# Twelve normalisations of a four-layer transformer kernel moved from blocks of their own into the blocks of the stages that read them

## The chip, the cores and the metric

The kernel runs on one core of one Trainium2 chip. The metric is the device time of one execution in microseconds (us), as the median of several runs. A core has five engines that run side by side and meet only at semaphores: TensorE (PE, with PEld for its weight loads), VectorE (DVE), ScalarE (ACT), GpSimd (POOL) and SyncE (SP), which here only issues DMA transfers.

## The reference

The input is x, 4 batches of 512 tokens with 128 channels, and a context of 154 tokens per batch. Four layers each add a cross attention and then a second part to x, and every such part reads a layer norm of x:

```python
def _layernorm(x, axis=-1, eps=1e-05):
    m = jnp.mean(x, axis=axis, keepdims=True)
    v = jnp.var(x, axis=axis, keepdims=True)
    return (x - m) / jnp.sqrt(v + eps)
...
x = x + _L0_xattn_ref(_layernorm(x, axis=-1), ctx_1024, itok_BxS_0_511, ...)
x = x + _L0_ffn_ref(_layernorm(x, axis=-1), ...)
```

The second part of layer 0 is a causal attention behind a convolution and a mixture of experts, each with one more layer norm (with gain and bias) in front. That of layer 1 is a soft decision tree. That of layer 2 is a latent attention and a mixture of experts, each behind an RMS norm with a gain. That of layer 3 is a product of 8-bit quantised matrices. This makes twelve norms.

## The kernel before

The whole of x lies in on-chip memory as X, with channels on the 128 partitions and 4 x 512 tokens along the free dimension. The norms write Y and Z of the same shape. All of it is float32. The program is a row of phases: input, window attention (names L0x), convolution and causal attention (L0f), experts (L0m), cross attention (L1x), tree (L1f), cross attention (L2x), latent heads (L2f), experts (L2m), attention over heads (L3x) and output.

Each phase is one `nc.Block`: an instruction stream for every engine, in the order in which it is written (or in which the phase's own order list `S.order` puts its steps). At its end `Phase.done` (L111) drains the engines, clears the phase's semaphores and makes all engines meet at a barrier. No scheduler moves instructions: each engine takes its stream in order and stops at the first wait that isn't met.

A norm is such a phase too, `phase_norm` (L179 to L253), which the stage calls through `norm((ld, loads))` just ahead of its own block. It works on four batches of 512 columns, one after the other on each engine:

- PE multiplies the source by a matrix of 1/128 (`mean`), L203, which leaves every token's mean in all partitions of banks 0 to 3 of the accumulator P. DVE subtracts it (L213).
- The squares are made by POOL (L242) for batches 0 and 2 and by DVE (L216, or L219 where nothing is centred) for 1 and 3. PE averages them (L206) into banks 4 to 7.
- ACT takes the logarithm of all four (L249), loads another function table, and takes exp(-0.5 x) of all four (L252).
- DVE multiplies (L227; L229 with a gain; L232 and L234 with gain and bias). Only when the last batch is done does the block end.

SP issues the weights of the following stage in the norm's block (`fetch`). The first norms of L0f and L2f are called from `build` and fetch nothing, so there the weights come with the second norm.

The stage's own block starts behind that barrier. What stands first in it, and is named below: in L0x, PE folds weights (L1196 on). In L0f, DVE clears tiles (L959, L960) and then starts the convolution (L968). In L0m and L2m, PE runs the router (L2147), 16 tiles of tokens with 4 or 8 outputs, DVE clears `hp` (L2209) and reads the logits (L2211, L2215). In L1x and L2x, POOL prepares the context (L526 to L529), DVE clears tiles and scales a bias (L652 to L658), and PE makes keys and values (L563, L564) and then queries (L556), which DVE reads at L677 and L665. In L1f, PE folds weights (L2305), ACT copies them (L2348), and PE multiplies Y by the copy (L2314). In L2f, PE folds weights (L1533, L1539), ACT copies them (L1629, L1631), and PE starts on Z (L1545), whose result DVE reads at L1674. In L3x, POOL clears tiles and ACT reads the keys and values (L2624) and queries (L2634). In the output phase, PE transposes Z (L2733) and DVE takes maxima (L2786).

Of the kernel before, what the change touches and what calls it, by code (L numbers as in the profile page):

```python
# [178 lines left out]
def phase_norm(nc, G, name, src, dst, center=True, gain=None, bias=None, fetch=None, sq=None):  # L179


    ph = Phase(nc, name)
    P = G["P"]
    xc = dst if center else src
    sq = rs = ph.sb("sq", [128, NB, T]) if sq is None else sq
    step, ld = ph.count("step"), ph.count("ld")
    given = [v for v in (gain, bias) if v is not None]
    cols = [ph.sb(f"col{n}", [128, 1]) for n in range(len(given))]
    gain, bias = ([c[:, 0:1] for c in cols] + [None, None])[:2]
    mean_up, cent, squared, squared_by_dve, var_up, ln, rstd, out = (  # L190
        ph.count(n) for n in ("mean_up", "cent", "squared", "squared_by_dve", "var_up", "ln", "rstd", "out"))
    with nc.Block() as block:
        @block.sync
        def _(sp):
            load_all(sp, ld, [(c[:], v) for c, v in zip(cols, given)])
            if fetch:
                load_all(sp, *fetch)

        @block.tensor
        def _(pe):  # L200
            if center:
                for b in range(NB):
                    nc.tensor.matmul(P[:, b, :], G["mean"][:], src[:, b, :], start=True, stop=True).then_inc(*mean_up.up())  # L203
            for b in range(NB):
                pe.wait_ge(*(squared_by_dve if b % 2 else squared).at(0, b // 2 + 1))
                nc.tensor.matmul(P[:, 4 + b, :], G["mean"][:], sq[:, b, :], start=True, stop=True).then_inc(*var_up.up())  # L206

        @block.vector
        def _(dve):
            if center:  # L210
                for b in range(NB):
                    dve.wait_ge(*mean_up.at(0, b + 1))
                    nc.vector.tensor_tensor(xc[:, b, :], src[:, b, :], P[:, b, :], ALU.subtract).then_inc(*cent.up())  # L213
                    if b % 2:
                        dve.wait_ge(*cent.at(0, b + 1))
                        nc.vector.tensor_tensor(sq[:, b, :], xc[:, b, :], xc[:, b, :], ALU.mult).then_inc(*squared_by_dve.up())  # L216
# [2821 lines left out]
```

## Time and profile before

| | us |
|---|---|
| median of 3 runs | 1771.7 |
| lowest and highest | 1768.62 and 1781.09 |
| the profiled execution | 1771.55 |
| its span, from its first to its last instruction | 1769.7 |

The mean granted clock of PE over that span is 0.873 of full speed.

So 1.85 us lie outside the span. The profile's page gives busy times per engine and the costliest groups. For this change the timeline is the view to read: it lists instructions by start and duration, with the time for which the engine had been idle and what it had waited for in brackets.

### The profile page before, as it was taken

The numbers are of one execution on the slowest core, as the hardware profiler recorded it, in microseconds if no ns is written. First come the engines' busy times: TensorE is split into PE (matmuls) and PEld (weight loads), VectorE is DVE, ScalarE is ACT, GpSimd is POOL, SyncE is SP. The second block draws the span as 40 slices with busy tenths as digits, with TensorE's granted clock in tenths as the row PEclk, the third lists the DMA queues.
The fourth block names the chain that finished last, engine by engine and source line by source line (L and its number), as shares of the span: only waits on it lengthen the run. The fifth ranks groups of instructions, "written<-read, shape, count | busy, mean of one in ns | idle before, by whom it ended". The sixth has DMA issues, their size and how long they took to land. (4 is left out here: it accounts for less than half of the span.)

```text
span 1769.7 us, 23757 instructions
## 1 busy us (share of the span) xinstructions
PE 1417.7 (80%) x8978; PEld 724.7 (41%) x8980; DVE 1041.1 (59%) x1468; ACT 704.1 (40%) x1306; POOL 572.9 (32%) x594
## 2 busy tenths in 40 slices
PE   5868755788858999699668986699999657689984
PEld 3345522333333444344234434354554232256553
DVE  3698736677642222578366752466676145468866
ACT  2444431666720000277334753244444221255522
POOL 1477713453302110332113301634422100047660
PEclk7789986899969999889886996899999669879986
DMA  3000010000010000100010002000000000000000
GB/s 102 0 1 0 1 44 1 1 1 1 1 75 0 0 0 0 50 1 1 9 49 1 1 1 44 1 1 1 2 2 1 1 29 0 6 1 1 2 1 26
DMA packets 19154, 20.58 MB, mean 12 GB/s; under 512 B 9803, under 2 KB 15163, under 8 KB 18408
## 3 DMA queue, kind: packets, MB, share of 16 engines
q1 hardware_dynamic: 18024, 19.07, 3.5%
q8 instruction: 71, 1.16, 0.3%
q14 instruction: 35, 0.29, 0.0%
q10 hardware_dynamic: 1024, 0.07, 0.0%
HBM read 17.94 MB, written 1.05 MB: 11 GB/s over the span
## 5 line engine op out<-in xcount | busy, mean ns | idle before, releaser
L1663 ACT ACTIVATE L2f_prob<-P 128x512 f32<-128x512 f32 x160 | 86.8, 595 | 112.6 <-PE P L1601 112.6
L998 DVE TENSOR_REDUCE L0f_nm<-P 128x2 f32<-128x768 f32 (+3 forms) x88 | 97.2, 1121 | 42.7 <-PE P L904 42.5
L2174 PE MATMUL P<-L0m_hm,L0m_w 128*128 128x512 f32 x256 | 112.5, 600 | 2.6 <-POOL L0m_hm L2136 2.6
L1691 DVE TENSOR_REDUCE L2f_nm<-P 128x2 f32<-128x768 f32 (+3 forms) x88 | 99.2, 1128 | 3.0
L1601 PE MATMUL P<-L2f_qs,L2f_ks 49*128 49x384 f32 (+3 forms) x512 | 94.3, 477 | 7.7 <-ACT L2f_prob L1663 3.9
L954 ACT ACTIVATE L0f_prob<-P 128x512 f32<-128x512 f32 x160 | 87.3, 601 | 29.4 <-PE P L917 26.9
L1517 POOL TENSOR_SCALAR_AFFINE_SELECT L2f_prob<-L2f_prob 128x512 f32<-128x512 f32 x64 | 39.7, 635 | 168.1 <-ACT L2f_prob L1663 168.0
L1690 DVE TENSOR_TENSOR P<-P,L2f_mask 128x256 f32<-128x256 f32 (+2 forms) x88 | 48.4, 550 | 74.3 <-PE P L1587 73.1
L1587 PE MATMUL P<-L2f_ks,L2f_qs 48*128 48x384 f32 (+3 forms) x512 | 87.7, 451 | 3.4 <-DVE L2f_nm L1691 3.4
L2516 POOL TENSOR_TENSOR L3x_exm<-L3x_exm,L3x_rec 128x2048 f32<-128x2048 f32 x16 | 72.3, 4526 | 26.1 <-DVE L3x_rec L2690 26.1
L2174 PEld LDWEIGHTS P<-L0m_hm,L0m_w 128*128 128x128 f32 x256 | 49.2, 193 | 64.9 <-issue 62.8
L1246 PE MATMUL P<-ident,L0x_pv 128*128 128x128 f32 x384 | 53.5, 305 | 24.4 <-POOL L0x_pv L1164 24.4
L1601 PEld LDWEIGHTS P<-L2f_qs,L2f_ks 49*128 49x128 f32 x512 | 49.4, 197 | 55.3 <-issue 41.4
L2198 ACT ACTIVATE L0m_ex<-P 128x512 f32<-128x512 f32 x16 | 9.6, 597 | 155.9 <-PE P L2174 155.9
L1154 POOL TENSOR_TENSOR L0x_prod<-L0x_qs,L0x_kg 128x1536 f32<-128x1536 f32 x20 | 68.5, 3454 | 3.3 <-ACT L0x_qs L1290 3.3
L1350 DVE TENSOR_REDUCE L0x_sc<-L0x_prod 128x16 f32<-128x1536 f32 x40 | 68.1, 1744 | 2.0 <-POOL L0x_prod L1154 1.9
L867 POOL TENSOR_SCALAR_AFFINE_SELECT L0f_prob<-L0f_prob 128x512 f32<-128x512 f32 x64 | 39.6, 637 | 88.6 <-ACT L0f_prob L954 88.6
L2251 DVE SCALAR_TENSOR_TENSOR L0m_rc<-L0m_ex,P 128x512 f32<-128x512 f32 x16 | 11.0, 688 | 95.0 <-ACT L0m_ex L2198 95.0
L2182 PE MATMUL P<-L0m_act,L0m_w 128*128 128x512 f32 x128 | 59.3, 623 | 9.2 <-DVE L0m_act L2254 9.2
L2574 PE MATMUL P<-L3x_exm,ident 128*128 128x512 f32 x128 | 62.5, 634 | 3.0 <-DVE L3x_rec L2690 1.9
L2136 POOL TENSOR_TENSOR L0m_hm<-Z,L0m_me 128x512 f32 x16 | 20.5, 1309 | 137.1 <-DVE L0m_act L2254 107.2
L1246 PEld LDWEIGHTS P<-ident,L0x_pv 128*128 128x128 f32 x384 | 51.3, 218 | 31.4 <-POOL L0x_pv L1164 29.7
(575 smaller groups left out, 3298.7 us busy)
## 6 DMA issues: line engine op xcount, KB each, us to landing
L0m_w<-in_L0m_w SPq DMA_DIRECT2D x1, 2048.0 KB, 7.7
L0f_va<-in_L0f_va SPq DMA_DIRECT2D x3, 512.0 KB, 4.7
in_xt<-in_x SPq DMA_DIRECT2D x1, 1024.0 KB
L0x_segi<-in_segb SPq DMA_DIRECT2D x1, 1024.0 KB, 5.0
L0m_w<-in_L0m_w SPq DMA_DIRECT2D x1, 1024.0 KB, 9.7
out<-out_o SPq DMA_DIRECT2D x4, 256.0 KB, 2.5
L1x_va<-in_va SPq DMA_DIRECT2D x3, 256.0 KB, 3.1
L1x_vr<-in_vr SPq DMA_DIRECT2D x3, 256.0 KB, 4.3
```

The lines of the kernel that those rows point to most:

```text
L954: nc.scalar.activation(S.group_prob(b, g)[:, slot, :], P[:, bank, :], ACT.Exp).then_inc(*S.act_done.up())
L998: nc.vector.tensor_reduce(S.nm[:, qt, first:first + 2 * many].rearrange("p (i e) -> p e i", e=2), P[:, bank:bank + 2, 0:many * width].rear ...
L1154: ops.tensor_tensor(prod[(k - 1) % S.NPROD][:], q, kg[b % 3][:, qt, j, :].unsqueeze(1).to_broadcast([128, H, 96]), ALU.mult)\
L1246: m = mm(P[:, bank, g * 128:(g + 1) * 128], pv[(4 * b + n) % 2][:, j, 4 * g:4 * g + 4, :].rearrange("p h c -> p (h c)"), G["ident"][:], st ...
L1350: nc.vector.tensor_reduce(sc[b % 2][:, n[0], n[1], :], prod[(S.place["prod", b, n] - 1) % S.NPROD][:], AX.X, ALU.add)\
L1587: m = mm(P[:, bank + e, p * width:(p + 1) * width], S.qs[b % 2][64 * e:64 * e + 48, pair, qt * 128:(qt + 1) * 128], S.ks[b % 2][64 * e:64 ...
L1601: m = mm(P[:, banks[e], at:at + width], S.ks[b % 2][64 * e:64 * e + 49, kt * 128:(kt + 1) * 128], S.qs[b % 2][64 * e:64 * e + 49, pair, q0 ...
L1663: nc.scalar.activation(S.group_prob(b, g)[:, slot, :], P[:, bank, :], ACT.Exp).then_inc(*S.act_done.up())
L1691: nc.vector.tensor_reduce(S.nm[:, qt, first:first + 2 * many].rearrange("p (i e) -> p e i", e=2), P[:, bank:bank + 2, 0:many * width].rear ...
L2174: m = mm(P[:, bank, :], lhs, hm[:, e, :], start=e == 0, stop=e == E - 1)
L2516: nc.gpsimd.tensor_tensor(ex[:], ex[:], S.rec[u % 2][:].unsqueeze(1).to_broadcast([128, H, 128]), ALU.mult).then_inc(*S.p_ready.up())
L2574: m = mm(P[:, 4, :], G["ident"][:], S.ex_of(b, n)[:, 8 * e + 4 * i:8 * e + 4 * i + 4, :].rearrange("p h q -> p (h q)"), start=e + i == 0, ...
```

## The change

`phase_norm` is gone. A class `Norm` holds the same instructions as methods, one for each engine (for DVE two: `dve_first` up to the squares, `dve_last` for the final products), and `Norms` runs one or two of them in a row. The stage calls these at the head of its own streams, so that the block end, the clearing of semaphores and the barrier between norm and stage no longer exist: 12 of 23 such meetings. What the barrier kept apart is now kept apart by waits: PE waits for all four logarithms (`N.ln`) before it writes an accumulator bank for the stage, and for `N.out` of batch b before its first step on that batch. Where a stage has two norms, the second's source waits per batch for the first's output, and they use two scratch tiles.

Some preparations move ahead of, or in between, the norm's parts:

- L0f: the clearing of tiles stands between `dve_first` and `dve_last` of the second norm.
- L0m, L2m: the clearing of `hp` likewise.
- L1x, L2x, L3x: POOL prepares the context before its squares. DVE clears tiles between `dve_first` and `dve_last`. In L1x and L2x its wait for all loads and the scaling of a bias stand there too.
- L0x: the one-hot tables, with their wait for the loads, stand between DVE's two parts.
- L2f: PE folds the weights between the two norms, ACT copies them there, and the loads are issued ahead of both norms.

```diff
-def phase_norm(nc, G, name, src, dst, center=True, gain=None, bias=None, fetch=None, sq=None):
...
-            dve.wait_ge(*out.at(0, NB))
...
-    ph.done()
+class Norm:
...
+    def source(self, eng, b):
+        if self.before is not None:
+            eng.wait_ge(self.before.out.sem, b + 1)
...
+class Norms:
...
+    def on_pe(self, pe):
+        for n in self.all:
+            n.on_pe(pe)
...
+    def dve_first(self, dve):
+        for n in self.all[:-1]:
+            n.dve_first(dve)
+            n.dve_last(dve)
+        self.all[-1].dve_first(dve)
+
+    def dve_last(self, dve):
+        self.all[-1].dve_last(dve)
```

In `phase_cross` (L1x and L2x), and in the same way in the other stages:

```diff
-    norm((ld, loads))
+    N = Norms(ph, G, norm)
     head_of = lambda g, j: 8 * (g // 2) + 2 * j + g % 2
     with nc.Block() as block:
+        @block.sync
+        def _(sp):
+            N.on_sp(sp)
+            load_all(sp, ld, loads)
...
             nc.gpsimd.tensor_copy(ctr[:], ctp[:, :, 128:PAD].unsqueeze(2).to_broadcast([128, NB, 4, 32])).then_inc(*ready.up())
+            N.on_pool(pool)
...
+            N.on_pe(pe)
             mm = nc.tensor.matmul
             pe.wait_ge(ld.sem, 16 * len(loads))
+            pe.wait_ge(N.ln.sem, NB)
             for s in S.order:
                 kind, b, n = s
                 if kind == "q":
+                    pe.wait_ge(N.out.sem, b + 1)
...
+            N.dve_first(dve)
             for t in S.qx:
                 nc.vector.memset(t[:, :, :, 48:64].rearrange("p t h c -> p (t h) c"), 0.0).then_inc(*cleared.up())
...
             dve.wait_ge(ld.sem, 16 * len(loads))
             link(dve, nc.vector.tensor_scalar(bq[:], bq[:], 8.0 ** -0.5, None, ALU.mult), step)
+            N.dve_last(dve)
```

In `phase_latent_heads` (L2f) and in `build`:

```diff
+            N.all[0].on_pe(pe)
             pe.wait_ge(ld.sem, 16 * len(loads))
...
             m.then_inc(*pre_full.up())
+            N.all[1].on_pe(pe)
+            pe.wait_ge(N.ln.sem, NB)
             for s in S.order:
                 kind, b, n = s
+                if kind in ("k", "p", "lat"):
+                    pe.wait_ge(N.out.sem, b + 1)
...
-        phase_norm(nc, G, "n2f", X, Y)
-        phase_latent_heads(nc, G, D, lambda fetch, sq: phase_norm(nc, G, "n2a", Y, Z, center=False, gain=D["L2_w_ln1"], fetch=fetch, sq=sq))
+        phase_latent_heads(nc, G, D, [(X, Y, {}), (Y, Z, {"center": False, "gain": D["L2_w_ln1"]})])
```

PE's stream at the start of L2f before, where `L2f_prob` is the second norm's scratch and the branches are the ends and starts of blocks:

```order
L203 MATMUL P<-X,mean 128x512 x4
L206 MATMUL P<-n2f_sq,mean 128x512 x4
L192 UNCONDITIONAL_BRANCH
L199 UNCONDITIONAL_BRANCH
L206 MATMUL P<-L2f_prob,mean 128x512 x4
L192 UNCONDITIONAL_BRANCH
L1529 UNCONDITIONAL_BRANCH
L1533 MATMUL P<-L2f_turned,L2f_qk 128x16 x16
L1539 MATMUL P<-L2f_qk,L2f_turned 32x128 x16
L1545 MATMUL P<-Z,L2f_wka 128x512
```

And the same place after the change, where L207, L1608, L1614 and L1624 are the new numbers of L206, L1533, L1539 and L1545:

```order
L204 MATMUL P<-X,mean 128x512 x4
L207 MATMUL P<-L2f_prob,mean 128x512 x4
L1608 MATMUL P<-L2f_turned,L2f_qk 128x16 x16
L1614 MATMUL P<-L2f_qk,L2f_turned 32x128 x16
L207 MATMUL P<-L2f_prob,mean 128x512 x4
L1624 MATMUL P<-Z,L2f_wka 128x512
```

The folding of the weights has moved from behind the second norm to the front of it, and four branches are gone.

DVE's stream at the start of L1x before, with L216 the squares of the norm and L227 its final products:

```order
L216 TENSOR_TENSOR n1x_sq<-Y 128x512
L227 TENSOR_TENSOR Y<-Y,n1x_sq 128x512 x4
L192 UNCONDITIONAL_BRANCH
L649 UNCONDITIONAL_BRANCH
L652 MEMSET L1x_qx 128x64x8 x2
...
L656 MEMSET L1x_kx 26x16x16
L658 TENSOR_SCALAR L1x_bq<-L1x_bq 128x128
L677 TENSOR_TENSOR L1x_xk<-P,L1x_bk 128x256
```

And after the change, where L237 and L248 are the squares and the products, and L698, L702, L704 and L724 the former L652, L656, L658 and L677:

```order
L237 TENSOR_TENSOR L1x_n0sq<-Y 128x512
L698 MEMSET L1x_qx 128x64x8 x2
...
L702 MEMSET L1x_kx 26x16x16
L704 TENSOR_SCALAR L1x_bq<-L1x_bq 128x128
L248 TENSOR_TENSOR Y<-Y,L1x_n0sq 128x512 x4
L724 TENSOR_TENSOR L1x_xk<-P,L1x_bk 128x256
```

The stage's preparations, with the wait for the loads that stands ahead of the scaling of `bq`, have moved in between the norm's squares and its products.

## Rows read from the trace of the kernel before

**Rows 1.** The page, first part: engine, busy us (share of the span), number of instructions.
```profile
PE 1417.7 (80%) x8978; PEld 724.7 (41%) x8980; DVE 1041.1 (59%) x1468; ACT 704.1 (40%) x1306; POOL 572.9 (32%) x594
```

**Rows 2.** Timeline, start of L0f: start us, duration us, engine, line, operation [idle before <-releaser].
```profile
245.76 6.23 PE L203 MATMUL P<-Y,mean 128*128 128x512 f32 x8 [6.20 <-PEq L111]
...
258.20 0.75 DVE L232 SCALAR_TENSOR_TENSOR Z<-Z,n0a_col,L0f_prob 128x512 f32<-128x512 f32 x1 [4.67 <-ACT L0f_prob L252]
...
264.15 0.48 DVE L959 MEMSET L0f_qk<- 128x512 uint32 x1 [1.13 <-PEq L111]
...
267.24 0.36 DVE L968 TENSOR_SCALAR L0f_hb<-Z,L0f_conv 128x512 f32<-128x512 f32 x1
```

**Rows 3.** Windows: stretch us, its length, busy of each engine, granted PE clock, DMA share, GB/s.
```profile
507.00:513.00 6.00, 0.00 (x0) 0.01 (x1) 4.68 (x8) 1.66 (x4) 0.00 (x0) 0.50 0.00 0
716.00:728.50 12.50, 7.24 (x16) 2.88 (x16) 6.77 (x10) 7.50 (x10) 2.08 (x2) 1.00 0.54 174
...
1087.00:1099.00 12.00, 11.33 (x67) 9.52 (x68) 0.35 (x1) 0.74 (x2) 1.90 (x2) 0.50 0.00 1
```

**Rows 4.** Timeline of PEld, start of L0x.
```profile
27.55 0.63 PEld L1196 LDWEIGHTS P<-L0x_wkT,L0x_wqT 64*48 64x48 f32 x7 [6.99 <-DMA L0x_kidx<-in_kidx]
```

**Rows 5.** Timeline, start of L0m.
```profile
507.20 0.75 DVE L232 SCALAR_TENSOR_TENSOR Z<-Z,n0m_col,n0m_sq 128x512 f32<-128x512 f32 x1 [4.74 <-ACT n0m_sq L252]
...
513.12 6.99 PE L2147 MATMUL P<-L0m_router,Z 128*128 128x4 f32 x32
520.47 0.91 DVE L2209 MEMSET L0m_hp<- 128x1024 uint32 x1 [7.16 <-PE P L2147]
```

**Rows 6.** Timeline, start of L1x.
```profile
721.54 1.38 SPq L130 DMA_DIRECT2D L1x_vr<-in_vr  x3
...
726.11 2.50 DVE L227 TENSOR_TENSOR Y<-Y,n1x_sq 128x512 f32<-128x512 f32 x4 [4.19 <-ACT n1x_sq L252]
...
731.13 1.19 PE L563 MATMUL P<-L1x_wkv,L1x_ctp 128*128 128x256 f32 x2 [7.72 <-POOL L1x_ctr L529]
...
733.29 0.42 DVE L677 TENSOR_TENSOR L1x_xk<-P,L1x_bk 128x256 f32<-128x256 f32 x1 [0.86 <-PE P L564]
```

**Rows 7.** DMA issues: tile, queue, count, KB each, median us to landing.
```profile
L1x_vr<-in_vr SPq DMA_DIRECT2D x3, 256.0 KB, 4.3
```

**Rows 8.** Timeline of ACT, start of L1f.
```profile
874.08 0.37 ACT L2348 COPY L1f_gw<-P 128x255 f32<-128x255 f32 x1 [3.19 <-PE P L2305]
```

**Rows 9.** Timeline, start of L2f.
```profile
1057.31 1.28 ACT L249 ACT_TABLE_LOAD   x1 [9.51 <-PEq L111]
...
1073.55 0.33 SPq L130 DMA_DIRECT2D n2a_col<-in_L_w_ln  x1
...
1074.67 6.51 PE L206 MATMUL P<-L2f_prob,mean 128*128 128x512 f32 x8 [7.27 <-POOL L2f_prob L242]
...
1082.34 1.39 SPq L130 DMA_DIRECT2D L2f_va<-in_L2f_va  x3
...
1083.95 2.74 DVE L229 SCALAR_TENSOR_TENSOR Z<-Y,n2a_col,L2f_prob 128x512 f32<-128x512 f32 x4 [7.34 <-ACT L2f_prob L252]
...
1087.67 6.98 PE L1533 MATMUL P<-L2f_turned,L2f_qk 32*128 32x16 f32 x32 [6.49 <-PEq L111]
...
1094.58 1.95 PE L1539 MATMUL P<-L2f_qk,L2f_turned 32*32 32x128 f32 x32
...
1098.64 0.69 DVE L1674 TENSOR_TENSOR L2f_ks<-P,L2f_ck 128x512 f32<-128x512 f32 x1 [11.95 <-PE P L1545]
```

**Rows 10.** Timeline of DVE, start of L2m.
```profile
1425.31 2.74 DVE L229 SCALAR_TENSOR_TENSOR Z<-Y,n2m_col,n2m_sq 128x512 f32<-128x512 f32 x4 [7.32 <-ACT n2m_sq L252]
...
1437.45 0.29 DVE L2215 TENSOR_TENSOR L2m_lg<-P,L2m_ebias 128x128 f32<-128x128 f32 x1
```

**Rows 11.** Timeline of ACT, start of L3x.
```profile
1553.12 0.37 ACT L2624 COPY L3x_xk<-P 128x256 f32<-128x256 f32 x1 [6.75 <-POOL L3x_va L2504]
```

**Rows 12.** Timeline of DVE, start of the output phase.
```profile
1744.63 0.69 DVE L2786 TENSOR_REDUCE out_amax<-P 128x4 f32<-128x512 f32 x1 [2.12 <-PE P L2733]
```

More of the change, by code:

```diff
@@ new lines, with __init__, on_sp, on_pe @@
+class Norms:
+    def __init__(self, ph, G, specs, sq=()):
+        self.all = []
+        for i, (src, dst, kinds) in enumerate(specs):
+            self.all.append(Norm(ph, G, src, dst, sq=sq[i] if sq else None, before=self.all[-1] if i else None, tag=f"n{i}", **kinds))
+        self.out, self.ln = self.all[-1].out, self.all[-1].ln
+    def on_sp(self, sp):
+        for n in self.all:
+            load_all(sp, n.ld, n.loads)
+    def on_pe(self, pe):
+        for n in self.all:
+            n.on_pe(pe)
+    def on_pool(self, pool):
+        for n in self.all:
+            n.on_pool(pool)
+    def on_act(self, act):
+        for n in self.all:
+            n.on_act(act)
+    def dve_first(self, dve):
+        for n in self.all[:-1]:
+            n.dve_first(dve)
+            n.dve_last(dve)
+        self.all[-1].dve_first(dve)
+    def dve_last(self, dve):
+        self.all[-1].dve_last(dve)
@@ L848, in phase_conv_attention, with _ @@
              (mask[:], D["mask_q"])] + [(t[:], D["L0f_va"]) for t in va]
-    norm((ld, loads), sq=S.prob[0][:, 0:NB, :])
+    N = Norms(ph, G, norm, sq=[t[:, 0:NB, :] for t in S.prob[0:2]])
     with nc.Block() as block:
+        @block.sync
+        def _(sp):
+            N.on_sp(sp)
+            load_all(sp, ld, loads)
         @block.gpsimd
         def _(pool):
+            N.on_pool(pool)
             for b, n in ((0, 1),):
@@ L1477, in phase_latent_heads @@
              (ck[:], D["L2f_ck"]), (sk[:], D["L2f_sk"]), (one[:], D["L2f_one"]), (mask[:], D["mask_q"])] + [(t[:], D["L2f_va"]) for t in S.va]
-    norm((ld, loads), sq=S.prob[0][:, 0:NB, :])
+    N = Norms(ph, G, norm, sq=[t[:, 0:NB, :] for t in S.prob[0:2]])
     with nc.Block() as block:
@@ L2125, in phase_experts, with _ @@
     hott_ps = [P[:, 1 + i, :].bitcast(BF16) for i in range(2)]
-    norm((ld, loads))
+    N = Norms(ph, G, norm)
     with nc.Block() as block:
+        @block.sync
+        def _(sp):
+            N.on_sp(sp)
+            load_all(sp, ld, loads)
         @block.gpsimd
         def _(pool):
+            N.on_pool(pool)
             if one:
@@ L2715, in phase_output @@
     tiles = lambda bank: P[:, bank, :].rearrange("p (t c) -> p t c", c=128)
-    norm((ld, loads))
+    N = Norms(ph, G, norm)
     with nc.Block() as block:
```

236 lines of the change are left out of this document (148 added, 88 removed).

## The prediction

> **What bounds the kernel now.** I read the page first, to see that no engine is full: PE is busy for 1417.7 us of the 1769.7 us span, DVE for 1041.1 [rows 1]. So the end is set stage by stage, and what the change is worth must be read where it acts, at the twelve norms. I read the timeline there. At each norm one finds the same serial chain over the engines (mean, subtraction, squares, mean, logarithm, table, exponential, product), then a barrier, then preparations of the stage that need no norm at all, and only then the first work on Y or Z. While the chain runs its four batches, most engines stand still. Last I read the windows for PE's granted clock, since PE's pieces there are short and follow idle time.
>
> The barrier's price is the bracket at the first instruction behind it: 1.13 us on DVE in L0f [rows 2]. Twelve go, about 12 x 1.1 = 13 us. The greater part must be what overlaps once they are gone. I follow, stage by stage, the first instruction of the stage that the rest hangs on, before and after. All of a stage is one pipeline behind it, so I let its shift reach the end in full.
>
> **L0x.** PE's first step in the stage waited for a DMA, not for the norm (6.99 us of idle, ended by `L0x_kidx` at 27.55) [rows 4]. The loads are issued no earlier. The gain lies between 0 and half a barrier, 0.6; I take 0.3. That DVE now makes the one-hot tables before Y costs nothing: PE first needs Y behind its folded weights.
>
> **L0f.** Two norms. PE started on the second at 245.76, after 6.20 us of idle that the barrier ended [rows 2]; so the first norm's means had ended at 239.6. A norm's first product starts some 2.8 us after its last mean (worked out at L2f) and takes 0.6, so the first Y is ready at 243.0, and PE may start on it 2.8 us earlier. The second norm's first product began at 258.20 after 4.67 us of idle. The clearing, from 264.15 to 267.24 = 3.1 us, fits into that idle time. The four products take the same 4.8 us (258.20 to 264.15 - 1.13 = 263.0), and the convolution then starts at once and not 267.24 - 263.0 = 4.2 us later. If PE still has its full clock when it restarts at 243, the means gain up to 2 us more; I count 0.5. Sum 7.5, bounds 7.0 and 9.0.
>
> **L0m.** The router took 6.99 us from 513.12 on and needs only Z of its batch. The first Z is ready at 507.20 + 1.2 = 508.4 [rows 5]. So it ends at 508.4 + 7.0 = 515.4, and DVE reads the logits 0.35 us later, at 515.8. Before, the clearing of `hp` stood in between and DVE read them at 520.47 + 0.91 = 521.4. Gain 5.6. At twice the clock the router would keep pace with DVE's products, which end at 512.0, and the gain would be 8.2. At least 5.0.
>
> **L1x and L2x.** Here DVE's products now stand behind its wait for all loads. The third `L1x_vr` is issued at 721.54 + 1.38 - 0.43 = 722.5 and lands some 4.3 us later [rows 6, 7], at 726.8, where the products started at 726.11 before. With the scaling of the bias they run from 727.1 to 729.6: the wait costs 1.0 us. PE's keys and values, which took 733.29 - 731.13 = 2.2 us at the low clock, are ready by 729.1. So DVE's L677 starts at 729.6 and not at 733.29: 3.7 us each, bounds 3.3 and 3.9. Queued behind the wait are the products, and PE's queries wait for them; they are needed only at L665, two DVE steps later.
>
> **L1f.** ACT had been idle for 3.19 us, since its last exponential, when it copied the folded weights at 874.08 [rows 8]. Now PE has them ready before: 3.2. PE's products on Y follow as before, or faster if the clock is still up. I take 3.5, bounds 3.2 and 5.0.
>
> **L2f.** The loads took from 1073.55 to 1082.34 + 1.39 to be issued, and landed about 2 us after that [rows 9], 12 us in all. They now start with the first norm, at 1057.3, and are there at 1069.3. The first norm's own PE work is over by then. PE folds weights: 6.98 + 1.95 = 8.9 us, to 1078.2. The squares of the second norm are made meanwhile. PE's second means take 6.51, to 1084.7; the first product came 1083.95 - 1081.18 = 2.8 us after their end, so at 1087.5; products and DVE's L1674 behind them: 1087.5 + 2.74 = 1090.2. Before: 1098.64. Gain 8.4. Here the new order puts the folding in front of the norm, in PE's queue and ACT's, so its speed decides: were folding and means at twice the clock, 7.7 us less, the gain would be near 15. I take 8.5, bounds 8.2 and 15.
>
> **L2m.** As L0m: the first Z at 1425.31 + 0.7 = 1426.0, 7.0 + 0.35 behind it: 1433.4 against 1437.45 [rows 10]. 4.0, bounds 3.8 and 7.5.
>
> **L3x.** ACT had been idle for 6.75 us, since its last exponential, when it read the keys [rows 11]. Now they wait there already, and POOL's clearing stands beside the norm. The queries, made from the first Y while ACT takes its other exponentials, come about in time for their place as ACT's fourth step. I take 6.5, bounds 5.9 and 6.7.
>
> **Output.** DVE was idle for 2.12 us between its last product and its first maximum [rows 12]; PE's transposition of batch 0 now lies beside the other products. 2.0.
>
> **The new waits.** Some 90 waits for `N.out` are added, nearly all met long before. The trace shows no price for a met wait. It lies between 0 and far less than the 1.13 us in which a whole barrier, with its drains and several semaphores, is passed [rows 2]. I take 0.01 each, 1 us, and at most 2.
>
> **Sum.** 0.3 + 7.5 + 5.6 + 3.7 + 3.5 + 3.7 + 8.5 + 4.0 + 6.5 + 2.0 = 45.3; less 1 is 44.3. By the profiled execution: 1771.55 - 44.3 = 1727.3. Its time is that of the median, 1771.7. The bounds add up to 40 and 62 us.
>
> **PE's clock** is the open term. The windows show it at one of two levels, 1.00 or 0.50 (2.4 or 1.2 GHz). In the norm of L1x it stayed at 1.00 from 716 to 728.5, though PE's 7.24 us of work lie at the front of that stretch and ended at 723.4 [rows 3]. In L0m it was at 0.50 all through 507 to 513 [rows 3], after means that had ended 2.8 us ahead of the first product, at 504.4 [rows 5]. So it fell within 2.6 us of the last wide matmul there, and later than 5 here. And 11.3 us of PE work on the weights of L2f, with 16 columns a matmul, did not raise it [rows 3]. In the changed kernel PE restarts 1.9 (L2f) to 4.1 us (L0m) after its means. I take the low level wherever the router or the folding runs.
>
> The Trainium skill (TensorE: Matmul & The Clock Gate, Seeing it yourself) shows a run in which the clock fell 5.2 us after the last matmul. The norm of L1x agrees with it, that of L0m does not. By that figure all the restarts above would find the full clock, and the sum would be near 60 us, the first rival's.
>
> **Rivals.**
> 1. *The clock stays up.* PE restarts soon enough that router, folding and means run at 1.00: 8.2 + 15 + 7.5 + 9 + 5 in place of 5.6 + 8.5 + 4 + 7.5 + 3.5 adds 15.6 us, 1712. For it: L1x kept the clock for 5 us. Against: L0m.
> 2. *Only the barriers go.* The stages' starts are bound by something that did not move (loads, or a slower batch behind the first), and the time comes to 1771.55 - 13 = 1758. For it: L0x, whose loads bound its start already. Against: in the other stages the bracket names the barrier, or PE work behind it.
> 3. *The change does not do what it says*, because an engine's first instruction of the stage waits for the norm's end all the same: 1771. In the new order of L1x, DVE's preparations do stand ahead of the products, so I hardly believe it.
> 4. *Slower: the rests were worth something.* If the granted clock inside the stages fell once the pauses are shorter, PE's busy time would grow. The profiled execution's mean clock is 0.873 by the span's summary, and 0.01 of it is about 1417.7 x 0.01 / 0.873 = 16 us where PE binds. From 0.845 on it eats the gain, and at 0.83 the kernel takes some 1790. For it: PE is the busiest engine. Against: in the rows the clock falls after idle time, never after work.
>
> **Chances.** The forecast 0.70, rival 1 0.17, rival 2 0.07, rival 3 0.03, rival 4 0.03. The range takes in rival 1 and half of the way to rival 2, as shifts may be lost further on: 1708 to 1744. A measurement tells about 1% (18 us) from no change: faster than that 0.88 (the forecast, rival 1, and 0.01 of rival 2), within it 0.09, slower 0.03.
>
> **What would show it.** In the profile after, no engine waits on the barrier between norm and stage. In L0f the first step of the convolution follows DVE's last product at once, and not 4.2 us later. In L0m the router starts 1.3 us after DVE's first product. In L1x and L2x DVE's products start a microsecond later behind the exponentials than before. In L2f the folding starts near 12 us after the phase's first table load, and DVE's L1674 comes 33 us after that load, not 1098.64 - 1057.31 = 41.3 [rows 9]. Wrong would be: a stage that from its first own work to its end has grown by what its start gained; a folding or router at the other clock level (that moves the sum to rival 1); a mean granted clock below 0.85.

## The result, and the profile of the changed kernel

The changed kernel took 1713.9 us (median of four runs, 1710.2 to 1717.4), against 1775.1 us (1768.6 to 1781.1) for the kernel before in the same comparison: ratio 0.9663, 95% interval 0.9628 to 0.9699. Compared twice more, unedited (below), it gave 0.9702 and 0.9690. All 14 runs lie between 1710.2 and 1726.5 us with a median of 1715.9. The forecast was 1727.3 with a range of 1708 to 1744: the direction was right and the mechanism held, as shown below; the gain was forecast some 11 us too small.

The page, first part: engine, busy us (share), number of instructions.

```profile
PE 1407.0 (82%) x8978; PEld 715.9 (42%) x8980; DVE 1041.5 (61%) x1468; ACT 704.1 (41%) x1306; POOL 574.1 (34%) x594
```

Against [rows 1] the instruction counts are the same and no engine but PE is busy for another time by more than 1.2 us, in a span of 1712.5 us, not 1769.7. PE and its weight loads (PEld) are busy for 10.7 and 8.8 us less with the same instructions, since more of them ran at the higher clock. The rest of the gain is less standing still.

To find where, I cut each profile at two marks per stage: the phase's first table load on ACT (every phase begins with it, behind the last remaining barrier), and the first instruction of the stage itself on the path, the same as in the prediction's steps. DVE's "keys" in L1x, L2x and L2f are its first step on the keys that PE has made. From the first mark to the second is the stage's *start*; from there to the next phase is its *rest*. In us:

| stage, second mark | start before | start after | forecast gain | gain | rest before | rest after |
|---|---|---|---|---|---|---|
| L0x, DVE's first step on keys | 41.3 | 41.2 | 0.3 | 0.1 | 176.9 | 176.8 |
| L0f, DVE's convolution | 35.0 | 27.2 | 7.5 | 7.8 | 227.3 | 230.1 |
| L0m, DVE reads logits | 26.8 | 19.6 | 5.6 | 7.3 | 194.7 | 192.9 |
| L1x, DVE's keys | 17.2 | 12.9 | 3.7 | 4.2 | 123.9 | 124.6 |
| L1f, ACT's first tanh | 21.1 | 16.9 | 3.5 | 4.2 | 32.8 | 33.3 |
| L2x, DVE's keys | 17.2 | 13.5 | 3.7 | 3.7 | 129.0 | 124.4 |
| L2f, DVE's keys | 41.3 | 32.2 | 8.5 | 9.1 | 316.3 | 308.9 |
| L2m, DVE reads logits | 22.5 | 15.8 | 4.0 | 6.8 | 97.4 | 96.2 |
| L3x, ACT reads keys | 18.3 | 11.4 | 6.5 | 6.8 | 175.0 | 180.5 |
| output, DVE's first maximum | 16.5 | 14.7 | 2.0 | 1.8 | 25.1 | 25.2 |
| sum | 257.2 | 205.4 | 45.3 | 51.8 | 1498.4 | 1492.8 |

The starts brought 51.8 us and the rests another 5.6, with terms from -5.5 to +7.4 where I had counted nothing.

L0f, the timeline that answers to [rows 2]:

```profile
232.32 1.28 ACT L221 ACT_TABLE_LOAD   x1 [5.45 <-PEq L111]
...
243.12 5.40 PE L204 MATMUL P<-Y,mean 128*128 128x512 f32 x8 [3.52 <-DVE Y L248]
...
250.11 0.48 DVE L1016 MEMSET L0f_qk<- 128x512 uint32 x1
...
254.76 0.75 DVE L250 SCALAR_TENSOR_TENSOR Z<-Z,L0f_n1col,L0f_prob 128x512 f32<-128x512 f32 x1 [1.48 <-ACT L0f_prob L224]
...
259.10 0.49 DVE L254 TENSOR_SCALAR Z<-Z,L0f_n1col 128x512 f32<-128x512 f32 x1
259.50 0.48 DVE L1027 TENSOR_SCALAR L0f_hb<-Z,L0f_conv 128x512 f32<-128x512 f32 x1
```

No row waits on a barrier between norm and norm, or norm and stage. PE's second means start on DVE's first Y, the clearing lies in DVE's wait for the exponential (1.48 us of it is left, of 4.67), and the convolution follows the last product at once.

L0m and L2m, the router (answering to [rows 5] and [rows 10]):

```profile
501.29 0.75 DVE L250 SCALAR_TENSOR_TENSOR Z<-Z,L0m_n0col,L0m_n0sq 128x512 f32<-128x512 f32 x1 [3.22 <-ACT L0m_n0sq L224]
...
502.62 6.46 PE L2239 MATMUL P<-L0m_router,Z 128*128 128x4 f32 x32 [0.49 <-DVE Z L254]
...
509.19 0.23 DVE L2306 COPY L0m_lg<-P 128x64 f32<-128x64 f32 x1 [2.93 <-PE P L2239]
...
1378.83 5.52 PE L2239 MATMUL P<-L2m_router,Z 128*128 128x8 f32 x32 [2.57 <-DVE Z L250]
...
1384.46 0.29 DVE L2310 TENSOR_TENSOR L2m_lg<-P,L2m_ebias 128x128 f32<-128x128 f32 x1 [3.54 <-PE P L2239]
```

The router starts 1.33 us after the first product in L0m, and takes 6.46 and 5.52 us. At the low clock it took 6.99 in L0m [rows 5], and 7.00 in L2m of `repeat` (below): part of it ran at the full clock here.

L1x (answering to [rows 6]):

```profile
707.15 1.38 SPq L130 DMA_DIRECT2D L1x_vr<-in_vr  x3
...
712.30 1.22 PE L607 MATMUL P<-L1x_wkv,L1x_ctp 128*128 128x256 f32 x2 [2.98 <-DMA L1x_vr<-in_vr]
...
712.54 2.50 DVE L248 TENSOR_TENSOR Y<-Y,L1x_n0sq 128x512 f32<-128x512 f32 x4
...
714.96 0.41 DVE L724 TENSOR_TENSOR L1x_xk<-P,L1x_bk 128x256 f32<-128x256 f32 x1
```

The last load is now what PE's keys wait for, and through the scaling of the bias DVE's products too. Keys and values are ready just when DVE is.

L2f (answering to [rows 9]):

```profile
1027.62 1.28 ACT L221 ACT_TABLE_LOAD   x1 [8.78 <-PEq L111]
...
1033.48 3.60 PE L207 MATMUL P<-L2f_prob,mean 128*128 128x512 f32 x8
...
1039.84 7.00 PE L1608 MATMUL P<-L2f_turned,L2f_qk 32*128 32x16 f32 x32 [2.76 <-DMA L2f_va<-in_L2f_va]
1039.85 3.34 DVE L248 TENSOR_TENSOR Y<-Y,L2f_prob 128x512 f32<-128x512 f32 x4 [4.67 <-ACT L2f_prob L224]
...
1046.77 1.95 PE L1614 MATMUL P<-L2f_qk,L2f_turned 32*32 32x128 f32 x32
...
1048.65 5.75 PE L207 MATMUL P<-L2f_prob,mean 128*128 128x512 f32 x8
...
1057.18 2.74 DVE L250 SCALAR_TENSOR_TENSOR Z<-Y,L2f_n1col,L2f_prob 128x512 f32<-128x512 f32 x4 [11.94 <-ACT L2f_prob L224]
1058.07 1.10 PE L1624 MATMUL P<-Z,L2f_wka 128*128 128x512 f32 x2 [3.67 <-DVE Z L250]
...
1059.83 0.68 DVE L1757 TENSOR_TENSOR L2f_ks<-P,L2f_ck 128x512 f32<-128x512 f32 x1
```

The folding starts 12.2 us after the table load (forecast "near 12") and DVE's first keys come at 32.2 (forecast 33, before 41.3).

### The profile page after: what moved, and what is told of

Same layout as the page of the kernel before. It is cut to its first block and busy times, and to the rows that moved or that the text cites. A ratio compares the mean times of both kernels' runs of the same rounds, so it can differ in the third digit from the quotient of the medians.

```text
span 1712.5 us, 23493 instructions
## 1 busy us (share of the span) xinstructions
PE 1407.0 (82%) x8978; PEld 715.9 (42%) x8980; DVE 1041.5 (61%) x1468; ACT 704.1 (41%) x1306; POOL 574.1 (34%) x594
## 5 line engine op out<-in xcount | busy, mean ns | idle before, releaser
L1680 PE MATMUL P<-L2f_qs,L2f_ks 49*128 49x384 f32 (+3 forms) x512 | 89.7, 456 | 8.3 <-ACT L2f_prob L1744 3.9
L2690 PE MATMUL P<-L3x_exm,ident 128*128 128x512 f32 x128 | 67.8, 679 | 3.0 <-DVE L3x_rec L2809 1.9
L1421 DVE TENSOR_REDUCE L0x_sc<-L0x_prod 128x16 f32<-128x1536 f32 x40 | 68.1, 1744 | 2.0 <-POOL L0x_prod L1213 1.9
L2225 POOL TENSOR_TENSOR L0m_hm<-Z,L0m_me 128x512 f32 x16 | 20.5, 1313 | 128.4 <-DVE L0m_act L2349 104.7
```

The costliest lines, as they stand in the source:

```text
L1421: nc.vector.tensor_reduce(sc[b % 2][:, n[0], n[1], :], prod[(S.place["prod", b, n] - 1) % S.NPROD][:], AX.X, ALU.add)\
L1680: m = mm(P[:, banks[e], at:at + width], S.ks[b % 2][64 * e:64 * e + 49, kt * 128:(kt + 1) * 128], S.qs[b % 2][64 * e:64 * e + 49, pair, q0 ...
L2690: m = mm(P[:, 4, :], G["ident"][:], S.ex_of(b, n)[:, 8 * e + 4 * i:8 * e + 4 * i + 4, :].rearrange("p h q -> p (h q)"), start=e + i == 0, ...
```

## The experiments

Eleven runs, in three groups, each group timed beside the kernel before. "The first profile" is that of the section above, and "the three profiles of the changed kernel" are this one and those of `repeat` and `repeat2`. Theory S stands for my account (overlap at the starts, chance of the clock in the rests), B for its rival (the barriers themselves), and R for the one that the change itself shifted the rests; other letters are told in the expectation that uses them.

**1. `repeat`: the changed kernel, unedited.**

> The changed kernel again, nothing edited. The first profile of it gained 51.8 us in the stretches from each stage's first table load to its first own work (forecast 45.3) and 5.6 us in the rests behind them (forecast 0), and these rests went from -5.5 us (L3x) to +7.4 us (L2f). Theory S (chance of the clock): the rests differ by where PE's granted clock happens to fall or rise in the bulk of a stage, which is another time in each execution. Then this profile has the same starts within 0.5 us and rests that differ from the first profile's by 2 us or more in at least three of the ten stages, and L2f's rest is not again 308.9. Theory R (the change did it): the new phase of the engines at the start carries on into the bulk, so every rest comes back within 0.5 us. Time by either: 1714 us, within 5.

Measured 1722.5 us (1714.5 to 1726.5), ratio 0.9702 (0.9665 to 0.9738). The windows of the rests of L2x, L2f and L3x (stretch, its length, busy of each engine, granted PE clock, DMA share, GB/s), first in the first profile after the change:

```profile
903.25:1027.62 124.37, 108.68 (x914) 52.90 (x912) 86.16 (x158) 78.00 (x120) 35.91 (x65) 0.90 0.00 1
1059.83:1368.71 308.88, 273.80 (x1821) 137.84 (x1819) 174.77 (x221) 123.96 (x236) 111.62 (x144) 0.96 0.01 1
1492.12:1672.60 180.48, 167.24 (x1937) 97.41 (x1936) 131.26 (x118) 80.57 (x111) 104.19 (x38) 0.87 0.01 2
```

and in `repeat`:

```profile
906.04:1035.23 129.19, 114.41 (x914) 55.30 (x912) 86.08 (x158) 78.13 (x120) 35.80 (x66) 0.84 0.00 1
1068.62:1386.35 317.73, 282.55 (x1822) 141.02 (x1821) 174.85 (x220) 123.97 (x237) 111.40 (x144) 0.94 0.01 1
1513.79:1684.62 170.83, 156.26 (x1937) 92.76 (x1936) 131.23 (x118) 80.31 (x111) 104.08 (x38) 0.95 0.01 2
```

It is the same program. DVE, ACT and POOL are busy for the same times to 0.3 us, PE is not, and the length goes with PE's busy time and against its granted clock: L3x takes 180.5 us at 0.87 and 170.8 at 0.95. So the -5.5 and +7.4 of the table are not the change's doing; theory R falls for these three stages. Of the part that starts agree to 0.5 us, L0f (+0.9), L2x (+0.6), L2f (+1.2) and L2m (+2.5) miss. In L2m this is again the clock; the router of `repeat`:

```profile
1397.46 7.00 PE L2239 MATMUL P<-L2m_router,Z 128*128 128x8 f32 x32 [2.57 <-DVE Z L250]
```

7.00 us where the first profile had 5.52. The starts of `repeat` gained 46.1 us in sum, those of the first profile 51.8; the forecast of 45.3 lies at the lower end. The time was 8.5 us over the 1714 that I expected, outside the 5 allowed.

**2. `all_four`: the waits per batch undone**, in all stages and in `Norm.source` for a second norm.

```diff
-                    pe.wait_ge(N.out.sem, b + 1)
+                    pe.wait_ge(N.out.sem, NB)
```

> The changed kernel, but every wait for the normalised batch waits for all four (in the stages, and in the second norm for the first). No barrier comes back, preparations stay. By the rows of the changed kernel's profile the first product stands 1.9 us ahead of the last one's end (3.5 where gain and bias are two instructions, in L0m). Theory S: it costs L0m 3.5, L2m 2.0, the second norms of L0f and L2f 1.9 each, L2f's keys 1.8, output 1.8, L1f 0.7, L3x 0 to 1.8, L1x and L2x 0 (keys and values go first and need no norm): 14.5 us, so 1728. Theory B (the gain is in the barriers that went, what overlaps behind them is hidden anyway): under 4 us, 1716.

Measured 1742.3 us (1742.0 to 1742.5), ratio 0.9829 (0.9802 to 0.9856), 20 us over `repeat` in the same group. Its starts sum to 222.9 us: 14.7 more than the mean 208.2 of the three profiles of the changed kernel, as expected (14.5). L0m has 4.1 of it. The rests, 1502.6 us, are 9.6 over the mean of those three profiles, so the time lost more than the starts did, and came 14 us over the 1728 expected; L1x's rest was 129.6 us in this profile, at a granted clock of 0.84, against 124.4 to 124.6 at 0.88 to 0.90 in those. Theory B, with its 4 us, falls: these waits are worth nearly as much as the barriers (run 5).

**3. `prep_behind`: the preparations behind the norm again.** Shown for L1x and L2x; likewise the other stages' clearing and one-hot steps on DVE, those on POOL, and in L2f the second norm's parts on PE and ACT ahead of the folding.

```diff
             N.dve_first(dve)
+            N.dve_last(dve)
             for t in S.qx:
...
-            N.dve_last(dve)
```

> The changed kernel, but DVE's and POOL's preparations stand behind their part of the norm again, and in L2f PE's and ACT's folding behind their part of the second norm. No barrier comes back, waits stay per batch, PE's preparations still stand beside the products. Theory S by the rows: L0f +3.1 (clearing between products and convolution), L1x and L2x +1.0 each (2.5 us of clearing behind the products, less the 1.8 us that the products now wait for loads), L3x +1.1, L0x 0 to 2.5 (three one-hot steps of 1.3 us), L0m 0 (0.91 us lies in the 2.9 us wait for the router), L2f near 0 (the folding lies beside the second norm's table load and exponentials): 7 us, 1721. Theory B: under 3 us. If the folding's place ahead of the second norm was what brought L2f's 9.1 us, L2f's start grows by 5 us or more.

Measured 1733.9 us (1729.6 to 1738.3), ratio 0.9773 (0.9743 to 0.9803). Starts 216.5 us, 8.3 over the mean of the changed kernel (expected 7). Of it L0f 2.9, L1x and L2x 2.3 and 1.8 (expected 1.0 each), L3x 2.3 (1.1), L0m 0; L2f became 1.8 *shorter* than the mean (30.8 against 32.2 to 33.4). But that is the clock:

```profile
1070.14 4.10 PE L1608 MATMUL P<-L2f_turned,L2f_qk 32*128 32x16 f32 x32
```

The folding stands straight behind the second means and straight ahead of PE's keys here, and took 4.10 us at a granted clock of 0.90, where it took 7.00 at 0.50 in the first profile. At the low clock the start would have been some 33.7 us (an estimate: 30.8 + 7.00 - 4.10), 1 us over the mean of the changed kernel. So the folding's place ahead of the second norm is worth about 1 us, and not the 5 that would have made it the source of L2f's gain; behind the norm it lies beside the table load and the exponentials. The time was 11.4 us over `repeat` in the same group, again more than the starts lost.

**4. `one_after_other`: both edits, and PE's preparations behind the products too.** What is left of the change is the absence of barriers, and loads issued at the phase's start.

```diff
-            pe.wait_ge(N.ln.sem, NB)
+            pe.wait_ge(N.out.sem, NB)
```

> The changed kernel with both edits of the two runs before, and PE's preparations wait for all four products too: each engine begins with the stage only behind the norm, as before the change, but through semaphores, without the twelve barriers. What is left of the change is the barriers. Theory S: 12 x 1.1 = 13 us faster than the kernel before, 1762. Theory B (a barrier costs more than its bracket, since it also drains every engine and restarts it): 1740 or less.

Measured 1746.1 us (1744.1 to 1749.7), ratio 0.9852 (0.9821 to 0.9883): 27 us faster than before, twice the 13. The starts say where: of 25.3 us, 9.9 lie in L2f, 15.4 in the other nine phases. Neither theory foresaw this. Of the 9.9, 2.3 are the clock's: the folding took 4.75 us here.

**5. `loads_late`: as 4, with the stage's loads of L0f and L2f behind the first norm, where they stood before.**

```diff
             N.on_sp(sp)
+            sp.wait_ge(N.all[0].out.sem, NB)
             load_all(sp, ld, loads)
```

> one_after_other (no barriers, but every engine begins with the stage behind the norm), and in L0f and L2f the stage's loads are issued only behind the first norm's last product, as in the kernel before. In one_after_other the starts of all stages were 25.3 us shorter than before the change, not the 13 that twelve barriers give at 1.1 us; 9.9 of them in L2f alone, where the loads need 12 us and are now issued with the first norm. Theory L (the loads' place is worth this): L2f's start grows from 31.5 by 7 us or more, L0f's by under 1, the kernel takes 1754, and what is left to the barriers is 16 us. Theory B (the barrier itself costs twice its bracket): L2f's start grows by under 2 us and the time stays at 1746.

Measured 1756.9 us (1752.2 to 1762.3), ratio 0.9905 (0.9868 to 0.9942). The timeline of L2f in it:

```profile
1057.35 1.28 ACT L221 ACT_TABLE_LOAD   x1 [8.76 <-PEq L111]
...
1072.12 0.33 SPq L130 DMA_DIRECT2D L2f_qk<-in_L2f_wqT  x1
...
1083.32 7.01 PE L1610 MATMUL P<-L2f_turned,L2f_qk 32*128 32x16 f32 x32 [3.20 <-DMA L2f_va<-in_L2f_va]
...
1094.32 0.69 DVE L1757 TENSOR_TENSOR L2f_ks<-P,L2f_ck 128x512 f32<-128x512 f32 x1 [8.68 <-PE P L1625]
```

L2f's start is 37.0 us, 5.5 more than in 4 (31.5); L0f's did not move. The loads land late and the folding waits for them, for 3.20 us; the other 2.3 us are the folding itself, 7.01 us at the low clock and not 4.75. Theory L holds against B, but short of the 7 us that it asked for, and only 3.2 us of it are the wait. What the barriers themselves are worth is what this kernel gains on the one before, 1773.37 - 1756.94 = 16.4 us by the medians of this group (10 to 23 by the interval); I had 13.

**6. `before_again`: the kernel before, unedited.**

> The kernel before, nothing edited, for a second profile of it. So far two profiles of the changed kernel and three of its variants gave rests (from a stage's first own work to the next stage's start) that differ although the instructions in them are the same: L2x 124.0 to 129.4, L2f 308.9 to 317.7, L3x 170.8 to 180.5. Theory S: the granted clock falls at other places in each execution, so this one too has at least two rests that differ by 2 us or more from the first profile of before (L0f 227.3, L2x 129.0, L2f 316.3, L3x 175.0), while its starts stay within 0.5 us where the clock is the same. Theory R (the change shifted them): all rests are those of the first profile of before within 0.5 us.

One run, 1771.8 us, and a miss for theory S: its windows are those of the earlier profile of that kernel, L3x excepted by 0.8 us.

```profile
929.11:1058.09 128.98, 114.79 (x916) 55.79 (x915) 85.88 (x157) 78.03 (x121) 35.91 (x65) 0.86 0.00 1
1099.33:1415.61 316.28, 282.30 (x1822) 140.92 (x1821) 174.94 (x220) 123.97 (x236) 111.61 (x144) 0.93 0.01 1
1553.81:1727.98 174.17, 160.40 (x1935) 95.00 (x1933) 129.96 (x116) 80.51 (x111) 104.18 (x38) 0.91 0.01 2
```

So an execution can repeat the clock's pattern closely. That it need not is shown by the kernel's other times (1766 to 1781 us) and by `repeat`. "Another time in each execution" was too strong: the rests of L2x and L3x take one of a few lengths.

**7. `warm`: three wide matmuls without a reader behind the norm's means in L0m and L2m, and behind the first norm's in L2f.**

```diff
             N.all[0].on_pe(pe)
+            pe.wait_ge(N.all[0].cent.sem, NB)
+            for _ in range(3):
+                nc.tensor.matmul(P[:, 3, :], G["mean"][:], G["X"][:, 0, :], start=True, stop=True)
```

> The changed kernel with three further matmuls of 512 columns on PE, whose result nobody reads, right behind the norm's means in L0m and L2m and behind the first norm's in L2f (2.75 us of work at the full clock, in idle time of 2.8 us or more). Theory C (the clock falls because PE rests there; rival 1 of the prediction): router at the full clock, L0m's start from 19.6 down by 2.3 us to where DVE's products bind, L2m's at 15.7 and not 18.2, and in L2f folding and second means at the full clock, 4.5 + 3.7 in place of 8.9 + 5.8 to 6.4 us, so its start falls by 6 us: 8 to 11 us in all, 1706 to 1709. Theory N (the folding with its 16 columns a matmul lets the clock fall whatever PE did before): L0m and L2m as above, L2f no better than 2 us; 3 to 6 us in all, 1711 to 1714. If the fillers only get in the way, the starts grow by up to 2.8 us each.

Measured 1720.3 us (1714.1 to 1722.5), ratio 0.9696 (0.9659 to 0.9732): no gain over the changed kernel, and above what either theory said (1706 to 1714). Windows of L0m in it:

```profile
499.70:502.50 2.80, 2.76 (x7) 0.95 (x5) 0.00 (x0) 2.60 (x5) 0.00 (x0) 1.00 0.90 380
502.50:504.00 1.50, 0.18 (x1) 0.09 (x1) 1.27 (x3) 1.50 (x4) 0.00 (x0) 1.00 0.07 22
504.00:507.00 3.00, 2.98 (x17) 2.97 (x17) 2.92 (x5) 0.11 (x1) 0.00 (x0) 0.62 0.00 0
507.00:510.50 3.50, 3.49 (x17) 3.40 (x16) 0.55 (x3) 0.00 (x0) 0.00 (x0) 0.50 0.00 0
```

The fillers fill the first stretch, the second is idle, and the router has the last two. The clock was full when the router began at 504.0 and fell in its first microsecond (0.62 over three us is 0.7 us at 1.00), with PE busy. The router took the same 6.46 us. Rival 1 of the prediction ("the clock stays up") is thus wrong for the router of L0m, though wide PE work ended only 1.6 us ahead of it. L2m's start was 16.2 us, where the three profiles have 15.8, 18.2 and 18.1. In L2f the start fell to 29.6 us and the folding from 7.00 to 4.77, the second means from 5.75 to 5.04, a gain of 2.6 to 3.8 us that lies between theory N (2 at most) and theory C (6). By sum of starts `warm` gained 4.3 us on the mean of the three profiles, within the scatter of the time.

**8. `split`: a semaphore of their own for the four loads that the first steps need, in L1x, L2x and L2f.** PE's keys, the scaling of the bias and the folding wait for `ld0`, later steps for `ld`.

```diff
-            load_all(sp, ld, loads)
+            load_all(sp, ld0, loads[:4])
+            load_all(sp, ld, loads[4:])
```

> The changed kernel, but in L1x, L2x and L2f the first four loads (what PE's keys and values, the bias that DVE scales, or the folding need) have a semaphore of their own, and the first steps wait for these alone. In the changed kernel DVE's products waited 1.8 us (L1x) and 2.4 us (L2x) behind the last load, and PE's folding in L2f 2.8 us. Theory S by the rows: starts L1x 12.9 to 11.3, L2x 13.5 to 11.7 and L2f 32.2 to 29.5 (to 27 if the folding catches the clock while it is up): 6 us, 1710. Rival: these loads land no sooner than the others (they share the DMA engines), then under 2 us.

Measured 1720.6 us (1713.8 to 1724.3), ratio 0.9696 (0.9656 to 0.9737). L2f's start is 28.8 us, L2x's 12.5 (from 13.0 to 14.1 in the changed kernel), L1x's 14.0, no better, since its first means ran at the low clock this time (5.21 us, where the changed kernel had 3.67). The time was 11 us over the 1710 expected. In L2f the folding now follows the means without a pause. The windows of means, folding, and what comes behind, in the changed kernel (with the pause as second row):

```profile
1033.50:1037.00 3.50, 3.50 (x9) 1.31 (x7) 1.47 (x3) 2.06 (x3) 1.04 (x1) 1.00 0.81 161
1037.00:1039.80 2.80, 0.08 (x1) 0.00 (x0) 0.00 (x0) 2.66 (x4) 0.00 (x0) 0.88 0.63 192
1039.80:1046.80 7.00, 6.96 (x34) 6.92 (x35) 5.38 (x6) 1.50 (x3) 2.84 (x2) 0.50 0.00 0
```

and in `split`:

```profile
1036.40:1039.90 3.50, 3.50 (x9) 1.32 (x7) 1.48 (x3) 2.06 (x3) 1.04 (x1) 1.00 0.61 150
1039.90:1044.70 4.80, 4.80 (x35) 4.75 (x34) 1.94 (x3) 4.16 (x6) 1.17 (x1) 0.75 0.34 105
```

With the pause the clock had fallen before the folding began, 2.1 us after the last wide matmul (0.88 over 2.80 us is 0.7 us at 0.50). Without it, half of the folding ran at the full clock, and it took 4.8 us in place of 7.0. That the pause made the clock fall is not shown. In both profiles the clock had been at 1.00 for 6.8 us when it fell (1032.3 to 1039.2 in the changed kernel, 1035.5 to 1042.3 in `split`), once with PE idle ahead of the fall and once with PE busy; the split brought the folding forward into that stretch.

**9 to 11. `repeat2`, `split3` (L0x's nine first loads split off too), `split3_warm` (with the fillers of 7 in L2f).**

```diff
-            load_all(sp, ld, loads)
+            load_all(sp, ld0, loads[:9])
+            load_all(sp, ld, loads[9:])
...
-            pe.wait_ge(ld.sem, 16 * len(loads))
+            pe.wait_ge(ld0.sem, 16 * 9)
```

> The changed kernel, nothing edited, beside the two runs that follow and for a third profile of it. The first two comparisons gave 0.9663 and 0.9702 of the kernel before; this one should lie between 0.964 and 0.973. Theory S: starts as in the two profiles (205.4 and 211.1 us in sum), while the rests of L2x, L2f and L3x take one of the values seen so far (124.4 or 129; 308.9 to 318; 170.8 to 180.5), not necessarily together.

> As split, and in L0x too the nine loads that PE's folding and ACT's copies need have a semaphore of their own. In the changed kernel PE stood 4.48 us in L0x until the last load had landed. By the rows the folding can start up to 4.4 us earlier there. PE's folding, POOL's table and PE's gathering follow one another without DVE's one-hot steps in between (these end at 32.7, the gathering starts at 44.8), so the start of L0x, 41.2, should fall by 3 to 4 us. With L1x, L2x and L2f as in split (starts 204.9 in sum) that makes 201.5: 3 to 9 us under the changed kernel in the same rounds, ratio to it 0.995 to 0.998. Rival: PE's folding in L0x comes to lie at the low clock and the gain is under 1 us.

> As split3, with the three matmuls without a reader in L2f between the first norm and the folding. In warm they took L2f's start from 32.2 and 33.4 to 29.6, but in split, without them, it was 28.8 already. Theory N (fillers only help where PE would wait for loads): they now stand in the way by up to 2.7 us and L2f's start grows to 29 or 31. Theory C (the clock is held up by them): folding and second means run at the full clock and L2f's start falls to 26 or less.

| kernel | median us | ratio to before | starts | rests |
|---|---|---|---|---|
| `repeat2` | 1716.4 (1711.5 to 1725.1) | 0.9690 (0.9663 to 0.9717) | 208.0 | 1487.1 |
| `split3` | 1714.7 (1704.2 to 1725.1) | 0.9671 (0.9637 to 0.9705) | 196.1 | 1500.1 |
| `split3_warm` | 1717.0 (1703.5 to 1717.7) | 0.9664 (0.9636 to 0.9692) | 197.8 | 1504.0 |

`split3` does at the starts what was expected. In L0x PE folds at once:

```profile
25.35 1.59 PE L1266 MATMUL P<-L0x_wkT,L0x_wqT 64*48 64x32 f32 x32 [0.87 <-ACT L0x_n0sq L221]
...
1034.93 4.81 PE L1612 MATMUL P<-L2f_turned,L2f_qk 32*128 32x16 f32 x32
...
1041.55 5.00 PE L207 MATMUL P<-L2f_prob,mean 128*128 128x512 f32 x8
```

so L0x's start fell from 41.4 to 37.4 us, and L2f's to 26.7. But 11.9 us at the starts against `repeat2` became 1.7 us in the medians, and the two intervals overlap: this version is not shown to beat the changed kernel, and the 3 to 9 us expected did not show. The rests of the profiled executions differ by 12.9 us the other way (L1x's alone is 128.4, not 124.6, L3x's 178.2, not 170.8). The fillers got in the way where no wait was left to fill: L2f 29.4, not 26.7. The folding itself was faster (4.03 us, not 4.81), but by less than the fillers' own 2.7 us. Theory N's side holds.

## Why the prediction was right, and where it was short

*The reading that decided it held.* The time was to be found at the norms, as overlap of the stage with the norm's serial chain, more than in the barriers. By the parts undone, one profile for each variant: the sum of the starts goes from 257.2 (before) to 239.6 without barriers (`loads_late`, -17.6), to 231.9 with L0f's and L2f's loads beside the first norm (-7.7, of which L2f 5.5, with the clock's 2.3 in it, and 2.0 in L0x, which that edit does not touch: there the first means of `loads_late` ran at the low clock, 6.62 us and not 3.67), to 208.2 with preparations beside the norm and waits per batch (-23.7). Undone singly these last two are worth 8.3 and 14.7, 23.0 together. So the waits per batch are the largest item after the barriers (17.6, or 19.7 without L0x), and rival 2 (only the barriers count, 1758) is what `loads_late` shows for the barriers alone: 1757.

*Step by step.* L0x (0.3, measured -0.1 to 0.2), L0f (7.5; 7.8, 6.8 and 7.8 in the three profiles), L1x and L2x (3.7 each; 3.9 to 4.2 and 3.0 to 4.2), L2f (8.5; 7.9 to 9.1), L3x (6.5; 6.8) and output (2.0; 1.6 to 1.8) came out as worked. The wait for the last load moved L1x's products from 9.98 to 10.50 us behind the table load, 0.5 and not 1.0. Too small were:

- **L0m**, 5.6, measured 7.2 to 7.3. I kept the first product at its distance from the phase's beginning, [rows 5]; it came 11.67 us behind the table load and not 12.63, since the means took 5.34 and not 6.39 us, and the router took 6.46, not 6.99. Both are the clock: 1.5 of the 1.7 us missed. I had taken the low level "wherever the router or the folding runs"; in part of the router it did not hold, and for the means I had left the clock out.
- **L2m**, 4.0, measured 6.8, 4.3 and 4.4. It is the forecast wherever the router ran low, and 2.4 more in the one execution in which part of it did not (1.5 in the router, 1.0 in the means, 5.40 us and not 6.39).
- **L1f**, 3.5, measured 4.2 in all three. ACT copies the folded weights 13.76 us behind the table load, 16.86 before: the 3.2 of the prediction. From there to the first tanh it is 3.1 us and no longer 4.3, and of this 1.1 I had taken 0.3. This too is the clock: PE's products on Y began at 1.00 (853.7 to 854.8 us) and at 0.50 before (874.7 to 878.3). I had named that case, and priced it too low.

In sum the starts gained 51.8, 46.1 and 49.2 us, against 45.3. This is the open term of the prediction, PE's clock: rival 1 would have added 15.6 us, and 1 to 6.5 came.

One reading behind that term was wrong. "11.3 us of PE work on the weights of L2f, with 16 columns a matmul" [rows 3] is 6.9 us of such work, 1.9 us with 128 columns, and at the end 2.5 us of products on Z with 512. The granted clock was 0.50 all through, as said.

*What adds up, and what was luck.* The three profiled executions took 1717.4 us in the mean, 9.9 under the forecast of 1727.3. Of this the starts brought 3.7 and the rests 5.4; 1.0 is the price that I had taken off for the waits, of which nothing is seen; against it, the first table load came 0.4 later. The 5.4 of the rests no term had forecast: they lie within what one execution differs from another, and fell on the lucky side.

*The new waits.* They were priced at 1 us. No run here shows a price for them apart.

*The rests.* I let each shift reach the end in full and expected nothing else. In the mean of the three profiles the rests were 5.4 us shorter than before (1493.0 against 1498.4), but over all eleven profiles of the changed kernel and its variants they lie between 1487.1 and 1506.0 without regard to the starts, and L3x's between 170.8 and 180.6. So the shifts reach the end on average, but one execution tells a sum of rests no closer than some ten us. Two rests do look like the change's own: L0f's is 228.6 to 230.7 in all eleven and 227.3 and 227.4 in the two profiles of before; L0m's is 192.6 to 192.9 in nine of them, 195.2 in the two whose PE begins with the stage behind all products (`one_after_other`, `loads_late`), and 194.7 in both of before. L0m's is the clock again: PE's four rounds of 32 wide matmuls there (`L0m_act`, `L0m_w`) take 13.99 or 14.00 us each, or 15.54 to 15.69 where the clock falls in one. It falls in two of the four before and in those two variants, and in one of the four in the nine. L0f's cause was not tried, and it is the sign of being wrong that the prediction named, in part: 2.8 us of rest against 7.8 of start.

*Slower (rival 4)* did not come: the mean granted clock was 0.884, above the 0.873 of before. Its price of 16 us per 0.01 does not hold between executions: `repeat2` has one of 1711.5 us at 0.888 and one of 1723.6 at 0.889.

The Trainium skill (TensorE: Matmul & The Clock Gate, Seeing it yourself) has a run in which the clock fell 5.2 us after the last matmul. The norm of L1x before the change agrees with it (at 1.00 until 5.3 us after PE's last work). Other rows of this case do not: 2.1 us in L2f of the changed kernel, and in L0m of `warm` 2.3 us after the last wide one (it ended at 502.5, and the clock fell at 504.7 of the trace), while PE ran the router. The prediction was right not to build its sum on that figure.

## What to carry to other kernels

Where a serial chain over the engines (a norm) comes ahead of a stage, the barrier is the smaller part of its price: look for the first instruction behind it that needs the chain's result, and only that, and let it wait for its own batch; then put loads and preparations beside the chain. One semaphore for all loads makes the first step wait for the last load, and what stands in one queue behind that wait, waits too; here splitting it came with starts 12 us shorter, part of it the clock's. And judge such an edit by the stretch it acts on in a profile as well as by the total: when PE's granted clock moves the rest by ten us from one execution to the next, a real gain of that size cannot be seen in a median of six runs.

## What the runs showed of the hardware that I had not expected

- In the same program a stage can take one of a few lengths, and the granted clock goes with it: L2x's rest 124.0 to 124.8 or 128.8 to 129.4 us in thirteen profiles of all kernels, nothing between; L3x's 170.8 (0.95), 174.2 to 175.9, 178.2 to 178.4 (0.88 and 0.89) or 180.5 and 180.6 (0.87). L2f's lie without such steps from 308.9 to 318.3. Between `repeat` and the first profile PE's busy time there went from 156.3 to 167.2 us, with 1937 records in both, and the length grew by 9.7.
- PE's clock can fall while PE is busy: 0.7 us after the router began, in `warm`. Against the prediction's own "in the rows the clock falls after idle time, never after work".
- DVE's four products and POOL's squares of the second norm, which overlap in L2f now, both took longer than alone: 3.34 us for the four at 1039.85, where L1x's took 2.50 at 712.54; POOL's 1.42 us each, against 1.04 alone:

```profile
1030.51 1.04 POOL L215 TENSOR_TENSOR L2f_prob<-Y 128x512 f32<-128x512 f32 x1 [1.94 <-DVE Y L231]
...
1040.62 1.42 POOL L215 TENSOR_TENSOR L2f_prob<-Y 128x512 f32<-128x512 f32 x1 [5.99 <-DVE Y L248]
```

  One by one, DVE's third product took 1.53 us and the other three 0.68 to 0.69. It began at 1041.06, while POOL's square ran to 1042.04, and ended 0.55 us behind it. The Trainium skill (SBUF — State Buffer, Terms) says that DVE and GpSimd share a pair of ports whose lock is exclusive and held for the full instruction, and that the loser "fully blocks". The rows fit that: the delay of the products lies in the one that began while POOL's square ran. No run here tries it.
